# The indirect writes of the slot list wait for the fifth block of the shared part

## What is computed

```python
ys = y * scale                                            # first layer
d = rsqrt(einsum('bi,io->bo', ys*ys, weight*weight) + EPS)
x = x + einsum('bsi,io->bso', x * ys[:, None, :], weight) * d[:, None, :]
...
shared = silu(xf @ w1) * (xf @ w3) @ w2                   # second layer, xf: [4096, 512]
s = sigmoid(concatenate([xf, tf], axis=-1) @ router_W)
_, topk_idx = top_k(s + router_bias, 2)
gates = s_sel / (s_sel.sum(axis=1, keepdims=True) + 1e-9)
h = gelu(einsum('nc,ech->enh', xf, W1e), approximate=False)
y = einsum('enh,ehc->enc', h, W2e)
routed = einsum('ne,enc->nc', combine, y)
x = x + (shared + routed) / 3
```

## Time and profile before

| What | Value |
|---|---|
| Median of 3 runs (lowest, highest) | 1239.59 us (1238.52, 1240.55) |
| Span of the profiled execution, first to last instruction | 1234.3 us |
| TensorE busy | 1127.2 us (91%), 5260 instructions |
| VectorE busy | 415.6 us (34%) |
| ScalarE busy | 334.1 us (27%) |
| GpSimd busy | 288.1 us (23%) |
| 64 indirect writes (L1028) | 62.2 us busy |
| 72 gathers (L1048) | 73.2 us busy |
| 71 scatters (L1061) | 111.7 us busy |
| Mean granted TensorE clock | 0.956 |

### The profile page before, as it was taken

One profiled execution on the slowest core, in us unless ns is written; L12 is line 12 of the kernel. 1 busy time (PEld: TensorE's weight loads), 2 busy tenths in 40 slices (PEclk: granted clock), 3 DMA queues, 4 the chain that ended last, 5 costly groups with the idle time before them and its releaser, 6 DMA issues. The chain is left out here.

```text
span 1234.3 us, 16122 instructions
## 1 busy us (share of the span) xinstructions
PE 1127.2 (91%) x5260; PEld 928.7 (75%) x5261; DVE 415.6 (34%) x647; ACT 334.1 (27%) x552; POOL 288.1 (23%) x319
## 2 busy tenths in 40 slices
PE   7999999992259999999999989999998799999992
PEld 6888888881148888888888878888887688888881
DVE  6554355571012333233222122333332133333330
ACT  4544442220012222222121122332322223323320
POOL 0000000047743232323330001132221122222232
PEclk9999999996569999999999999999999899999996
DMA  5777676654047767777752138754378744434533
GB/s 184 253 251 256 245 273 239 239 213 146 1 160 249 273 236 269 263 250 274 264 179 75 44 103 310 235 93 76 77 225 275 244 85 81 85 77 77 93 60 42
DMA packets 66364, 218.24 MB, mean 177 GB/s; under 512 B 8416, under 2 KB 9568, under 8 KB 55040
## 3 DMA queue, kind: packets, MB, share of 16 engines
q1 hardware_dynamic: 29072, 134.09, 30.5%
q0 software_dynamic: 23248, 56.52, 19.7%
q10 hardware_dynamic: 14016, 27.27, 6.6%
HBM read 121.57 MB, written 96.87 MB: 177 GB/s over the span
## 5 line engine op out<-in xcount | busy, mean ns | idle before, releaser
L412 PE MATMUL banks<-xh,w13h 128*128 128x512 f32 x512 | 201.1, 393 | 16.7 <-issue 16.7
L414 PE MATMUL banks<-xh,w13l 128*128 128x512 f32 x512 | 201.0, 393 | 15.0 <-issue 15.0
L413 PE MATMUL banks<-xl,w13h 128*128 128x512 f32 x512 | 200.8, 392 | 12.6 <-issue 12.6
L775 DVE TENSOR_TENSOR gm<-sil,banks 128x512 f32<-128x512 f32 x64 | 44.0, 687 | 335.5 <-ACT sil L599 333.7
L599 ACT ACTIVATE sil<-banks 128x512 f32<-128x512 f32 x64 | 38.2, 597 | 411.6 <-PE banks L414 319.6
L485 PE MATMUL banks<-we,hidth 128*128 x284 | 119.5, 421 | 12.3 <-issue 12.3
L1028 POOL DMA_INDIRECT slots_d<-rec,sadr x64 | 62.2, 972 | 279.1 <-DVE sadr L873 259.9
L1061 POOL DMA_INDIRECT out<-ys,six x71 | 111.7, 1573 | 65.2 <-POOL six L1057 40.1
L412 PEld LDWEIGHTS banks<-xh,w13h 128*128 128x128 f32 x512 | 96.9, 189 | 38.9 <-issue 19.2
L414 PEld LDWEIGHTS banks<-xh,w13l 128*128 128x128 f32 x512 | 96.9, 189 | 36.0 <-issue 16.2
L413 PEld LDWEIGHTS banks<-xl,w13h 128*128 128x128 f32 x512 | 96.9, 189 | 35.7 <-issue 16.0
(11 more groups left out here) (145 smaller groups left out, 1655.6 us busy)
## 6 DMA issues: line engine op xcount, KB each, us to landing
we_d<-ehl SPq DMA_DIRECT2D x32, 1024.0 KB
we<-we_d SPq DMA_DIRECT2D x16, 2048.0 KB, 8.6
xs_d<-xs POOLq DMA_DIRECT2D x36, 512.0 KB, 5.0
xg<-xs_d ACTq DMA_DIRECT2D x36, 512.0 KB
eraw<-expert_w SPq DMA_DIRECT2D x32, 512.0 KB
xin<-xT SPq DMA_DIRECT2D x8, 1024.0 KB, 6.5
x1t_d<-x1t SPq DMA_DIRECT2D x8, 1024.0 KB, 8.8
x_d<-x1tok ACTq DMA_DIRECT2D x8, 1024.0 KB, 9.1
```

Of the source, the lines that this page charges most:

```text
L412: pe.matmul(ps[hc % 2][:, :], w_hi, xh[:, j, c, :], start=(c == 0), stop=False)
L413: pe.matmul(ps[hc % 2][:, :], w_hi, xl[:, j, c, :], start=False, stop=False)
L414: last = pe.matmul(ps[hc % 2][:, :], w_lo, xh[:, j, c, :], start=False, stop=(c == DC - 1))
```

## The change

Two waits are put ahead of GpSimd's first indirect write.

```diff
             pool.wait_ge(pads_in, 48)
+            pool.wait_ge(ab_done, 4 * HC + 2)
+            pool.wait_ge(gl_ready, 4 * HC + 1)
             for k in range(K):
                 pool.wait_ge(sadr_done, k + 1)
                 for i in range(NT):
```

## The result

The changed kernel takes 1267.2 us (median of 4 runs, 1261.9 to 1274.4) against 1239.1 us (4 runs, 1233.1 to 1240.6). The ratio is 1.023, with a 95% interval of 1.020 to 1.026 (1.0197 at its lower end): slower, clear of noise, but not with certainty by 2% or more. The profiled execution has a span of 1267.4 us; before it was 1234.3. So 33 us more are to be found in the spans.

The account below looks back on a forecast made before the run. The prediction took the expert part's chain of scatters as the bound: first scatter 768 + chain 459.2 + end 8.8 = span 1236.0, plus 5.3 gives 1241.3 us; range 1224 to 1270, slower 0.63.

Parts of the forecast that it names:

- the likeliest case: Whole kernel: TensorE's lost time goes, gathers end later, scatters run shorter; 1241.3 us (1229 to 1254), chance 0.52.
- the rival in which the hole moves: TensorE's block 4 loses 72.9 us instead, first scatter at 785, time 1263 us; chance 0.28.
- the hole: TensorE's near-idle stretch near 300 us, while GpSimd issues 64 indirect writes and TensorE's loop makes its first pass: 72.9 us lost.
- What goes: 72.9 us: TensorE near 300 us: the whole lost time vanishes and later blocks run that much earlier; bounds 0 to 72.9 us.
- The rival's own reason: TensorE's loop, not just its first pass, meets trouble beside the writes, so the second pass loses 72.9 us; chance 0.28.
- The row on code fetches: Instruction queue taken for TensorE's: 4 packets from 356 to 445 us, 1 in the next 298 us; weighed against the moved-hole rival.
- When the writes start, and the first gather: GpSimd: first indirect write at 410.1 us, first gather at 497.3 us instead of 345.55.
- When the gathers end: GpSimd's gather pairs and stores end later beside weight loads, putting the first scatter at 768 us; bounds 750 to 793.
- a weight load at 2.65 us: Delay charged to GpSimd's gathers per 2 MB weight load beside them; seven cost 18.5 us, bounds 0 to 6.2 each.
- The chain: Expert part's 71 scatters, nearly each waiting for the previous landing: 459.2 us instead of 475.0, with 15.75 saved.
- From span to time: End of the forecast: 5.3 us added to the 1236.0 us span, giving 1241.3 us.
- The slack: Between GpSimd's last store at 646.77 and first scatter at 750.52, which waited for ys: about 100 us.

Follow-up runs that it names:

- the run in straight code: The kernel before with TensorE's blocks 2 and 3 written out and its loop holding blocks 4 to 7: 1238.9 us.
- the late version with waits: The changed kernel with a wait for the landing after every 8 of GpSimd's indirect writes: 1277.0 us, span 1275.2.
- the run with the delay alone: The kernel before, early writes kept, with one wait ahead of the first gather for block 4's fourth chunk: 1269.3 us, span 1267.5.

## Why the prediction was right, and where it wasn't

The direction and the range held: slower had 0.63, and 1267.2 lies in 1224 to 1270. But the likeliest case was not the one that came. What came was the rival in which the hole moves, which had 0.28 and gave 1263. "Slower" was right for the wrong reason, and that 1263 lies only 4 us from the 1267 measured is partly luck, as the terms below show.

*What goes: 72.9 us.* This is the step that failed. The hole came back in block 4 with 65 us. The reason I gave was that TensorE ran without a gap from 360 us on, beside gathers and in its first pass. Those gathers are pairs with pauses of 3 to 10 us behind each, and in the run with a wait after every 8 writes TensorE kept going as well (1.1 us lost), beside writes and in the same first pass. Whether it is the pause that does it is not shown. I took a difference of series for a difference of passes.

*The rival's own reason* was wrong as well. It held the loop responsible. In straight code the hole was as deep. The row on code fetches is true and had no bearing: the run in straight code has a hole with no back branch at all on TensorE. By the Trainium skill (Runtime: NRT & Kernel Launch, Instruction fetch mechanics) a taken branch out of the two pages at hand forces a fetch, from which I made a fetch in every pass; but the same section gives TensorE an instruction memory of 128 KiB, or 2048 instructions, against 32 KiB for most engines. A pass of the loop has 16 chunks of 36 matmuls with as many weight loads, 1152 instructions (an estimate from the counts in the trace), and would fit. The trace agrees with the larger memory: one packet in the second and third pass. I weighed a rule against a row where neither spoke of the cause.

*When the writes start, and the first gather* (410.1 and 497.3) came out at 411.6 and 498.0.

*When the gathers end.* For the moved hole I had the first scatter at 785, and it came at 786.3. The agreement hides two errors that cancel. The gathers got on faster at first: 15 periods lie between the first store and the one at 622.74, where I had 13.3 by 624.5. And I priced a weight load at 2.65 us. The five periods from 721.89 to 780.43 took 58.5 us, 26.7 more than five alone; six loads were issued from 720.0 to 773.0, and with 3 us for the output store (my own term, no row shows it by itself) each cost about 3.9. The forecast's own case shows it too. In the late version with waits the first gather was 18.5 us later than foretold (515.8), since the waits stretch the series of writes, so 786.5 was due for the first scatter. It came at 797.0.

*The chain.* 459.2 us foretold, 472.2 measured, 469.2 in the late version with waits. Its first five periods took 32.9 us (786.28 to 819.16) against 45.5 before and 29.7 foretold, but the other 65 took 439.4 against 429.5. Of these 9.9 us, 7.8 lie in the ten periods beside the eight weight loads in the middle (913.85 to 1009.62, 95.8 us against 88.0); why they cost more is not shown. I subtracted at one end and held the rest for fixed. With the 10.5 us of the loads and the 469.2 of the chain my own case would have had a span of 1256.5, not 1236.0.

*From span to time.* I added 5.3 us, from a median and a span of different runs. The profiled run of the changed kernel took 1269.15 us with a span of 1267.4, so 1.8 are enough. The moved hole's 1263 was thus a span of 1258 that came out at 1267.4; the chain is what it missed by.

*The slack.* I saw the 100 us in front of the first scatter and spent them rightly: 152 us of delay, 104 of slack, and a part paid back by transfers that meet less traffic. That sum, and not the hole, sets the result; the run with the delay alone has the same span as the changed kernel.

## What to carry to other kernels

Before moving work out of the way of a stall, find out what the stall follows: halve the suspected series, break it up, and put the victim into other code. Here a few waits for landings within the series took 66 us off in the one run where the hole stood, and cost nothing measurable in the twelve where it didn't, while the delay pushed 72 gathers behind the point where their slack ended. An engine at 23% busy can still hold the schedule, through everything that is queued behind its first wait.

## What I had not expected of the hardware

A series of GpSimd's indirect transfers without a break, one each 1.26 us, slowed TensorE 18 us after its first in the kernel before (260.34 to 278.86) and 26 us after it in the changed one (411.61 to 437.46). For most of the hole a matmul comes every 2.8 us instead of every 0.23, while the DMA engines stand nearly idle (1 GB/s). What reaches the others is late as well. In the kernel before, the 24th matmul of the second chunk of block 2 has this row in TensorE's timeline:

```profile
282.38 0.39 PE L414 MATMUL banks<-xh,w13l 128*128 128x512 f32 x1 [0.80 <-issue]
```

The silu that needs it starts at 355.91, 73 us on. With series of 10 us the silu lose 1.1 us in all, which is the zero of this count. Above that zero a series of 20 us cost some 6 us, one of 40 us 24 to 27 (but only about 11 where it was the second), one of 81 us 64 to 74. Reads did it as well (71). Each figure is of one profiled run with the hole. And the kernel before, with the same 64 writes in one series, took 1168.2 and 1165.5 us on two other chips (26 runs) in place of 1236 to 1239. So the same program took 70 us more in one place than in another, and a comparison needs the kernel before on the same chip and at the same time. What makes the difference is open.
